# First attention: the next batch's turned rows leave PSUM ahead of the residual's normalisation and the exponentials

## The reference, cut to what matters

```python
def _L0_xattn_ref(q, k, v, Wq, bq, Wk, bk, Wv, bv, Wff, bff):
    qp = q @ Wq.T + bq ; kp = k @ Wk.T + bk ; vp = v @ Wv.T + bv   # one head of 256
    scores = jnp.einsum('bhqd,bhkd->bhqk', qp, kp) * scale
    scores = jnp.where(causal[None, None, :, :], scores, -jnp.inf)
    attn = jax.nn.softmax(scores, axis=-1)
    out = jnp.einsum('bhqk,bhkd->bhqd', attn, vp)
    out = out.transpose(0, 2, 1, 3).reshape(B, T, C)
    return out @ Wff.T + bff
...
x = x + jnp.tanh(g_xattn[0]) * _L0_xattn_ref(_layernorm(x), ctx_1024, ctx_1024, ...)
x = x + jnp.tanh(g_ffn[0]) * _L0_ffn_ref(_layernorm(x), ...)      # 8 experts, top 2, capacity
x = x + jnp.tanh(g_xattn[1]) * _L1_xattn_ref(_layernorm(x), ctx_1024, ctx_1024, ...)
x = x + jnp.tanh(g_ffn[1]) * _L1_ffn_ref(_layernorm(x), ...)
return x
```

## Time and profile before

| | us |
|---|---|
| median of 3 runs | 988.31 (987.16 to 988.34) |
| the profiled execution: its own time | 982.83 |
| its span, first to last instruction | 981.1 |
| the first attention within it, to the last instruction of its gate | 0 to about 188 |

### The profile page before, as it was taken

How to read it: one execution, slowest core, us unless ns; L and a number is a source line. 1 busy time by engine, 2 the same in 40 slices (tenths; PEclk the granted TensorE clock), 3 DMA queues, 4 the chain that set the end, 5 groups by cost and what they waited for, 6 DMA issues and landing times. The chain is left out here.

```text
span 981.1 us, 15352 instructions
## 1 busy us (share of the span) xinstructions
PE 670.2 (68%) x4856; PEld 494.8 (50%) x4856; DVE 519.2 (53%) x1701; ACT 428.3 (44%) x847; POOL 333.3 (34%) x473
## 2 busy tenths in 40 slices
PE   3878887215599989998923487877778411576765
PEld 3766776113477766776722244545545310354544
DVE  1354453271755476545302567778764368656551
ACT  1333323003565577556511265565656210455562
POOL 1323332115165334644222153444443110342422
PEclk9997898556799999999975697898878655687887
DMA  5132131225255424541221122222201030344431
GB/s 166 45 112 71 64 109 44 77 94 161 52 138 141 120 66 94 140 129 17 25 46 38 39 79 67 77 75 76 67 24 39 27 112 0 114 121 111 122 85 22
DMA packets 74955, 78.66 MB, mean 80 GB/s; under 512 B 8101, under 2 KB 66513, under 8 KB 74641
## 3 DMA queue, kind: packets, MB, share of 16 engines
q1 hardware_dynamic: 62305, 62.11, 19.8%
q0 software_dynamic: 10928, 15.57, 9.3%
q10 hardware_dynamic: 1664, 0.27, 0.2%
HBM read 54.99 MB, written 22.94 MB: 79 GB/s over the span
## 5 line engine op out<-in xcount | busy, mean ns | idle before, releaser
L1630 DVE CUSTOM_DVE_ANT_0 c_sn<-c_ps_s,k_mask 128x128 f32<-128x128 f32 (+1 forms) x256 | 75.8, 352 | 55.9 <-PE c_ps_s L1768 55.8
L1154 PE MATMUL b_ps_y<-b_w2h,b_hh 128*128 128x256 f16 x320 | 88.9, 278 | 10.1 <-DVE b_xl L1036 9.9
L1154 PE MATMUL b_ps_y<-b_w2h,b_hl 128*128 128x256 f16 x320 | 88.8, 277 | 0.0
L1154 PE MATMUL b_ps_y<-b_w2l,b_hh 128*128 128x256 f16 x320 | 88.7, 277 | 0.0
L910 POOL DMA_INDIRECT res<-b_y,b_s_idx x40 | 71.5, 1787 | 45.6 <-ACT b_y L950 36.0
L896 POOL DMA_INDIRECT b_xg<-rows,b_g_idx x40 | 39.9, 997 | 135.3 <-DVE b_g_idx L1054 125.5
L1462 POOL TENSOR_SCALAR_AFFINE_SELECT c_pr<-c_pr 128x512 f32<-128x512 f32 x64 | 43.2, 676 | 112.7 <-ACT c_pr L1521 111.7
L1026 DVE TENSOR_TENSOR b_hl<-b_h,b_hh 128x640 f16<-128x640 f32 x64 | 52.8, 825 | 35.9 <-ACT b_hh L933 35.7
L1796 PE MATMUL c_ps_v<-c_pr,k_vx 128*64 128x256 f32 (+1 forms) x512 | 64.2, 378 | 5.6 <-POOL c_pr L1462 5.0
L1121 PE MATMUL b_ps_h<-b_xh,b_w1h 128*128 128x320 f16 x256 | 57.5, 307 | 13.0 <-ACT b_h L928 12.2
L1521 ACT ACTIVATE c_pr<-c_ps_t 128x768 f32<-128x768 f32 x64 | 51.7, 807 | 16.0 <-PE c_ps_t L1782 16.0
(11 more groups left out here) (382 smaller groups left out, 1819.3 us busy)
## 6 DMA issues: line engine op xcount, KB each, us to landing
b_w<-in_L_ffn_W_dram SPq DMA_DIRECT2D x16, 1024.0 KB, 7.7
d_w<-in_L_ffn_W_up_dram SPq DMA_DIRECT2D x8, 682.0 KB
d_w<-in_L_ffn_W_down_dram SPq DMA_DIRECT2D x8, 640.0 KB
k_ks<-kT SPq DMA_DIRECT2D x48, 64.0 KB, 2.7
c_qs<-q SPq DMA_DIRECT2D x48, 64.0 KB, 2.3
rows<-a_rows SPq DMA_DIRECT2D x8, 264.0 KB, 2.3
rows<-c_rows SPq DMA_DIRECT2D x8, 264.0 KB, 2.2
a_x_in<-in_x_dram SPq DMA_DIRECT2D x8, 256.0 KB, 2.9
```

What stands on the lines that cost most here:

```text
L1154: last = pe.matmul(ps_y[(j + CT) % 2][:, 0:D], a, b[:, f, :], start=(f == 0 and k == 0), stop=(f == FC - 1 and k == 2))
L1630: dve.tensor_tensor_reduce(sn[r][:, a:b], ps_s[:, r, a:b], mask[:, a:b], -1.0, 3.0e38, ALU.add, ALU.min, mx[g % 2][:, q, r, j:j + 1]).then ...
```

## The change

On ScalarE the copy of `ps_x` into `xT` for batch n+1 (with its two waits) moves from the start of step n+1 to the middle of step n, behind `vp` of batch n and ahead of the normalisation of the residual and of the two exponentials. Batch 0's copy stands ahead of the first step. No instruction is added or removed on any engine, and the programs of the other engines stay as they are.

```diff
+            def turned(n, u):
+
+                after(act, s_ptx, n)
+                after(act, s_ps, n, 2)
+                act.activation(xT[u][:], halves(ps_x), ACT.Copy).then_inc(s_xT, 1)
+
+            turned(0, 0)
+
             def step(n, u, front, back, gate):
                 m, v, g = n - 1, 1 - u, n - 2
                 if front:
-                    after(act, s_ptx, n)
-                    after(act, s_ps, n, 2)
-                    act.activation(xT[u][:], halves(ps_x), ACT.Copy).then_inc(s_xT, 1)
                     after(act, s_pq, n)
...
                     after(act, s_po, n, 2)
                     act.activation(vp[u][:], halves(ps_w), ACT.Copy).then_inc(s_vp, 1)
+                    if has_next(n):
+                        turned(n + 1, v)
                 if back:
```

## The result

| | before, us | after, us |
|---|---|---|
| median, runs taken beside each other | 987.73 (985.2 to 988.34, 4 runs) | 949.87 (946.67 to 954.0, 4 runs) |
| the profiled execution: own time / span | 982.83 / 981.1 | 954.0 / 952.3 |

The ratio is 0.9624, 95% interval 0.9582 to 0.9665: 37.9 us, or 3.8%, faster. The forecast was 954.4, 33.9 us faster, in a range of 950 to 963. The range was stated from a kernel before of 988.31 us; the ratio applied to that gives 951.1 us, inside it. Where the surplus of about 4 us comes from was the first question of the study.

What follows compares the result with a forecast made beforehand. TensorE was taken to bound the first attention, its largest hole being the wait for ScalarE's copy. Step 1's 2.3 us plus 31.6 in steps 2 to 7 make 33.9; 988.3 less 33.9 is 954.4 us, range 950 to 963.

Steps and rivals of the forecast that it cites:

- The bound and the hole: First attention: TensorE bounds it, and its largest hole is the wait for ScalarE's copy `xT`, 20.8 us in six times.
- 1.38 us from turn to ps_q: Every step: `ps_q` starts 1.38 us after the input's turn starts, as in step 0, where nothing was in ScalarE's way.
- The stretch of 6.65 us: Steps 2 to 7, turn's start to `ps_v`: 6.65 us each, 39.9 in all instead of 71.5, a gain of 31.6.
- The 0.1 us put down for `x1T`: Steps 2 to 7: 0.1 us added per stretch because the logits may wait for `x1T` from ScalarE in alternate steps.
- The rest of 6.87 us: Each step from `ps_v` to the next turn: 6.87 us of dense TensorE work at full clock, unchanged.
- Step 1, 2.28 us: Step 1: `ps_q` starts at 39.04 instead of 41.32, saving 2.28 us at the same full clock.
- No part of the saving depends on the 5.5 us between the profile and the median: Whole kernel: runs' median is 5.5 us above the profiled execution; the saving was claimed independent of that difference.
- The clock's term, 12.7 us: Steps 2 to 7: 12.7 us of the saving is low TensorE clock behind the holes that would go.
- The cover of 0.5 us on ScalarE: ScalarE: the moved copy ends about 0.5 us before `nmr` releases the residual's normalisation, so moving it costs nothing.
- The cover of 1.3 us on VectorE: VectorE: `v1` is made at 10.5 us behind the turn, and VectorE must be free at about 11.8, leaving 1.3 us.
- The rival that the clock would not come back: First attention: `ps_q` stays at low clock and only holes go, saving 21.2 us, 967.1 in all; chance 0.07.
- The rival of the input's chain: Steps 2 to 7: late input loads use up `v1`'s cover, giving about 960 or 968 us; chance 0.10.

Runs made afterwards that it cites:

- second profile: The changed kernel measured and profiled once more without any edit: 949.89 us, ratio 0.9623 to the kernel before.
- small `kl`: Changed kernel with GpSimd's subtraction cut to 8 columns of each chunk, the rest of kl zero: 963.10 us, ratio 0.9639 to the kernel before.
- copy half way: Against the changed kernel, the copy stands behind the residual's normalisation but ahead of the exponentials: 972.28 us, ratio 0.9853 to the kernel before.
- the holes were filled with work: Kernel before plus five matmuls with overwritten result behind the turn of the context, steps 1 to 7: 971.03 us, ratio 0.9833 to the kernel before.
- three copies of 1.02 us together: Changed kernel plus three unused ScalarE copies between the moved copy and the residual's normalisation: 951.42 us, ratio 0.9632 to the kernel before.
- later loads: Changed kernel plus two 256 KB stores ahead of each next-input load in steps 1 to 6: 969.45 us, ratio 0.9705 to the kernel before.

## Why the prediction was right, point by point

*The bound and the hole.* Right. The wait that was named is the one that went; its idle time moved to ScalarE.

*1.38 us from turn to ps_q.* 1.31 to 1.33 us in all seven steps. *The stretch of 6.65 us*: 6.51, 6.66, 6.59, 6.66, 6.70 and 7.34, in sum 40.46 instead of 39.9. Right to 0.6 us. The 0.1 us put down for `x1T` was right in size only: no row shows TensorE waiting for `x1T` in steps 2 to 7, and the time went ahead of the turn of the residual, which in steps 3, 5 and 6 starts 1.95 to 1.99 us behind `ps_q` instead of 1.83. Step 7 lost another 0.6 us at the same place (1.1 in the second profile), because VectorE was late with x1 beside GpSimd's work; with the small `kl` that wait is gone. *The rest of 6.87 us* did not move.

*Step 1, 2.28 us.* In the first profile it was 14.42 less 12.07, 2.35: right for that execution, and mis-sized for the kernel. In the two other profiles of before step 1 took 17.11 us, so it is worth 5.0 us. With the 1.1 us of the steps behind it, this is 3.75 us that the first profile did not have, as much as the forecast's shortfall of 4.0 us in the first comparison and more than that of 1.9 in the second. The step that failed is the sentence "0.31 and 2.59 us of idle time ahead of `ps_q` cost no clock": I took one case of 2.59 us for a property of the hole's length. The runs show that a hole of 2.50 to 2.67 us costs the clock in 8 of 9 cases. The same reading was then carried into the expectation for the copy half way, and failed there in the open.

*No part of the saving depends on the 5.5 us between the profile and the median.* Not borne out, and for the same reason. The two further executions of the kernel before took 7.5 and 4.7 us longer than the first. 3.7 and 4.2 us of it were a later start-up, which has nothing to do with the change; another 3.75 were low clock in the loop, which the change removes; the later stages took the rest (0.1 us more, 3.3 us less).

*The clock's term, 12.7 us.* Right: 13.3 us in the loop and 14.6 in time when the holes were filled with work. The rival that the clock would not come back fell.

*The cover of 0.5 us on ScalarE.* Right in kind, and too small: 0.67 to 1.29 us in the first profile, and three copies of 1.02 us together nearly fitted in. I had counted the cover from the copy's end and left out that the normalisation started somewhat behind `nmr` before as well.

*The cover of 1.3 us on VectorE.* Mis-sized, and not one number: VectorE still waited 0.49 and 1.19 us for the output in steps 2 and 4, and not at all in steps 3, 5 and 6, where `dl`, `zt` and `oh` together ran 1.7 to 1.9 us longer than in step 4, beside GpSimd's work; in the second profile step 4 had no such wait either. The rival of the input's chain did not come true by itself; with the statistics 3.2 to 5.3 us later it decides, at 0 to 2.6 us a step and 7.3 in all, where my price, 1 us for the first 2.3 and then one for one, would have said 1.9 to 4.0 a step and 14 in all.

*The later stages.* From the next stage's first load to the end of the span it is 789.7 us before and 789.9 after in the first profiles, 783.9 to 792.5 in eight others on chips of the same speed, of either order: the saving went through whole, under a scatter of a few us.

## What to carry to other kernels

Where the engine that bounds a stage has its longest hole, look at what its releaser was doing in that time; if it was standing at the head of its queue for something later, the two can be exchanged, and the cover is the idle time that remains behind the moved instruction. Price TensorE's idle time twice: once for itself and once for the low clock of the matmuls behind it, here 20.1 us for itself, and 13.3 us for the clock in one profile and 17.1 against the other two. Take a second profile before calling a hole harmless, since one case says little of what the clock will do.

## What the runs showed of the hardware that I had not expected

Equal holes ahead of equal work cost the clock in one case and not in the next: 1.77 us in 4 of 7 steps of one execution, 2.50 to 2.67 us in 8 of 9 over four profiles. The clock can also fall within the work behind the hole, as the turn and the logits of step 8 show. With low clock the eight records of `ps_q` took 3.4 to 3.8 us, with full clock 1.99.

A short VectorE instruction took as long as the GpSimd instruction beside it: `oh`, twice 128x16 elements, 1.22 us for both beside the subtraction of 1.15 us and 0.28 us without it. Packing the steps brought the two together; in the kernel before they never met. The larger copy `prT` (0.53 us) was not lengthened beside the same subtraction before the change, so it is not every VectorE instruction. Not only `oh` is drawn out: `zt` took 1.25 us beside GpSimd's `xb` of 1.27 us in the kernel with later loads, and 0.23 us in step 1 there; each time the VectorE instruction ended within 0.2 us of the GpSimd one. Which forms are held up and which are not, the runs leave open.

The start-up ahead of the first attention's loop scatters by 4 us between executions of the same program, 37.66 to 41.87 us in three of the kernel before, with part of the work on the folded weights done now at one clock and now at the other (a turn of a weight matrix in 0.60 us or in 1.06).
